# Attention heads of a graph layer: exponentials copied by DMA into float32r tiles and transposed from there, ScalarE's order changed

## The chip, the cores and the metric

The kernel runs on one core of one Trainium2 chip. The metric is the device time of one execution in microseconds, the median of several runs. A core has TensorE (PE, matmuls and transposes; its weight loads are shown apart as PEld), VectorE (DVE), ScalarE (ACT), GpSimd (POOL) and SyncE (SP), which here only issues DMAs. SP's DMAs go through one queue over the core's 16 DMA engines.

## What is computed

A two-layer graph attention network over 1,250 nodes with 768 features, then a feed-forward block. All in float32. The stage that the change touches is the attention of the first layer, with 8 heads of 128 channels:

```
h = (layernorm(x) @ W1.T).reshape(n, 8, 128)
e = leaky_relu(a_src[src] + a_dst[dst], 0.2)        # per edge and head
ex = exp(e - segment_max(e, dst)[dst])
alpha = ex / (segment_sum(ex, dst)[dst] + 1e-16)
h1 = relu(segment_sum(alpha[:, :, None] * h[src], dst) + b1)
```

The second layer does the same with one head of 768 channels on `h1 @ W2.T`; the block behind it is a normalisation and two matmuls with a GELU, and for six rows a routed variant.

## The kernel before, in words

The edges are first counted into a dense 1,250 x 1,250 matrix of log counts, `LC`. A head is then dense work on 10 row tiles of 125 destination nodes by 1,250 source nodes: the segment sum is a matmul of the features with the transposed matrix of exponentials.

The head stage walks over 40 pairs of row tiles (8 heads of 5 pairs; `NG` is 5, `n` counts pairs through all heads, `hh` counts head pairs). What is done for one pair k is spread over the steps of four engines:

- DVE, `logits` (L1824, L1832): for each of the two tiles, source logit plus destination logit with the leaky ReLU into `L[r]`, then adding `LC` with the row maximum; L1836 makes the negated maxima. Four tiles `L` serve two pairs. Then `reciprocals` of pair k-1 and `multiply` (L1860) of pair k-3.
- ACT: `evac` of pair k-1 (L828, five copies of 500 columns from PSUM into `PT`), then `exp` of pair k (L815, in place in `L[r]`, with row sums), `rdb_copy` of pair k-2 (L845), `relu` of pair k-4 into `hT` (L856).
- PE: `turn_bank` of pair k-1 (L1219: 20 transposes of 125 x 125, each a weight load of a block of `L` and a pass of the identity, into five PSUM banks), `spread` of pair k-2 (L1256, two transposes), `aggregate` of pair k-2 (L1240: 10 float32 matmuls, which the profile shows as 20, features `h1s` against `PT`).
- SP: a load of the next head's source logits (`load_logits`, L442, into `asb`, 1,250 KB) and of its features (`load_features`, L437, into `h1s`, 560 and 65 KB).

All order is written out by hand; engines meet only at semaphores: `exp_done` (exponentials of a pair), `tb_full` (a bank turned), `tb_evac`, `agg_done`, `mul_done`. An `L` tile is free for the pair after next when its pair is turned:

```
                    if not (first and k < 2):
                        dve.wait_ge(tb_full, NG * n + -NG)
```

Around the stage, SP's list holds six loads of `w2n_sb` (L409, 512 KB each) just before the head loop, and the load of `w2_sb` (L479, 3,072 KB), the second layer's weights, just behind it. In the stage's sixth step (the seventh pair's logits) PE multiplies `w2n_sb` (L1275). After pair 39 ACT splits `w2_sb` into a high part (L881, 8 casts), then does the last `rdb_copy` and `relu` and makes the first tiles `h1Tt_hi` (L885); PE starts the second layer on them (L1311).

## Time and profile before

| | us |
|---|---|
| median of 3 runs | 733.01 (731.76 to 735.08) |
| profiled execution, span | 730.7 |
| PE busy in the span | 718.9 |
| DVE busy | 518.6 |
| ACT busy | 390.7 |

The profile is one execution; its span runs from the first to the last instruction, and nothing else of its own time is recorded. Busy times of the page are shares of the whole span. Three views are used below: windows (busy time of each engine in a stretch), the timeline (instructions in order of time, like neighbours merged), and one line's or all lines' instructions with their lengths. In timeline rows the first number is the start, the second the length of the merged stretch; "x20" is the count. Times are microseconds from the span's start, mean lengths nanoseconds.

### The profile page before, as it was taken

What the parts mean: (1) busy time and instruction counts of PE and PEld (TensorE: products, weight loads), DVE (VectorE), ACT (ScalarE), POOL (GpSimd) and SP (SyncE); (2) the same over time, 40 slices, a digit from 0 to 9 for tenths busy, and PEclk for the clock granted to TensorE, in tenths of its full rate; (3) what the DMA queues carried; (4) which work ended last, traced back from release to release, by engine and by line L of the source; (5) the groups of instructions that cost most, each with busy time, mean ns of one, the idle gap of its engine ahead of it and who ended that gap; (6) DMA issues with size and microseconds to landing.
All of it is one profiled execution on the core that took longest, in us unless ns stands there. A gap on an engine that the chain in (4) does not pass through costs nothing.

```text
span 730.7 us, 13048 instructions
## 1 busy us (share of the span) xinstructions
PE 718.9 (98%) x4607; PEld 655.4 (90%) x4607; DVE 518.6 (71%) x940; ACT 390.7 (53%) x749; POOL 112.2 (15%) x95
## 2 busy tenths in 40 slices
PE   8899999999999999999999999999999999999998
PEld 6699999789899999999999999999999898978965
DVE  5899888699999999999999452336567543717141
ACT  4665574388698889888888931122231413322100
POOL 2569330000000000000000000000233330222211
PEclk9999999999999999999999999999999999999999
DMA  8627655759121221302230020001873544215011
GB/s 284 206 81 213 190 165 153 191 164 333 37 71 36 71 61 45 105 21 85 76 132 0 0 57 1 1 0 36 259 255 90 174 136 156 92 61 175 22 37 49
DMA packets 39665, 78.92 MB, mean 108 GB/s; under 512 B 4074, under 2 KB 25392, under 8 KB 38721
## 3 DMA queue, kind: packets, MB, share of 16 engines
q1 hardware_dynamic: 33932, 60.53, 27.2%
q10 hardware_dynamic: 4500, 13.82, 5.8%
q0 software_dynamic: 1184, 3.92, 1.8%
q8 instruction: 30, 0.49, 0.3%
q14 instruction: 19, 0.15, 0.1%
HBM read 62.97 MB, written 15.29 MB: 107 GB/s over the span
## 4 chain that ended last, share of the span: by engine, by line
PE 94%; DMA 3%; ACT 1%; DVE 1%; issue 0%; ACTq 0%; SPq 0%; POOL 0%; POOLq 0%; DVEq 0%
PE bank L1240 23%; PE bank L1382 15%; PE bank L1219 12%; PE bank L1311 12%; PE bank L1117 11%; PE bank L1458 5%; PE bank L1478 5%; DMA w1n_sb<-in_W 3%; PE bank L1034 3%; PE bank L1363 1%; PE bank L1256 1%; PE bank L1036 1%; PE bank L1430 1%; PE bank L1446 1%; PE bank L1049 1%; PE bank L1493 1%
## 5 line engine op out<-in xcount | busy, mean ns | idle before, releaser
L1240 PE MATMUL bank<-PT,h1s 125*128 125x250 f32 x800 | 175.8, 374 | 0.0
L1240 PEld LDWEIGHTS bank<-PT,h1s 125*128 125x128 f32 x800 | 148.5, 190 | 15.7
L1824 DVE SCALAR_TENSOR_TENSOR L<-asb,nadh 125x1250 f32<-125x1250 f32 x80 | 118.0, 1517 | 3.1 <-PE bank L1219 1.3
L828 ACT COPY PT<-bank 125x500 f32<-125x500 f32 x200 | 99.8, 596 | 37.8 <-PE bank L1219 37.8
L1832 DVE CUSTOM_DVE_ANT_0 L<-L,LC 125x1250 f32<-125x1250 f32 x80 | 113.4, 1455 | 0.0
L815 ACT ACTIVATE L<-L,nm 125x1250 f32<-125x1250 f32 x80 | 107.8, 1371 | 0.0
L1219 PEld LDWEIGHTS bank<-ident,L 125*125 125x125 f32 x800 | 93.3, 189 | 3.9 <-ACT L L815 1.5
L1219 PE MATMUL bank<-ident,L 125*125 125x125 f32 x800 | 94.6, 273 | 0.7 <-ACT L L815 0.7
L2005 DVE TENSOR_TENSOR x2f<-bank,x2f 125x384 f32<-125x384 f32 x20 | 10.3, 552 | 63.4 <-PE bank L1478 63.4
L1641 DVE TENSOR_TENSOR hotr<-iota,r 125x1500 f16<-125x1500 f16 x50 | 46.5, 931 | 8.0 <-PE bank L1036 4.4
L646 POOL MEMSET pick<- 128x90 f32 x1 | 0.2, 168 | 277.8 <-ACT hT L856 277.8
L1382 PE MATMUL bank<-h_hi,PT_hi 125*125 125x384 f32 x200 | 42.1, 352 | 0.0
L890 ACT CAST h_hi<-bank 125x384 f32 (+1 forms) x20 | 8.6, 483 | 59.6 <-PE bank L1311 59.6
L1382 PE MATMUL bank<-h_lo,PT_hi 125*125 125x384 f32 x200 | 40.4, 341 | 0.0
L916 ACT ACTIVATE L<-L,nm 125x1250 f32<-125x1250 f32 x10 | 13.4, 1339 | 50.3 <-DVE nm L1969 50.2
L1900 DVE COPY as2c<-bank 125x1 f32<-125x1 f32 x10 | 1.6, 158 | 54.4 <-ACT h_hi L890 54.4
L1478 PE MATMUL bank<-fc_sb,gT 128*125 128x384 f32 x120 | 40.2, 486 | 0.0
L1458 PE MATMUL bank<-yT,fc_sb 128*128 128x250 f32 x180 | 39.2, 375 | 0.7 <-ACT yT L930 0.7
L1382 PE MATMUL bank<-h_hi,PT_lo 125*125 125x384 f32 x200 | 38.3, 337 | 0.0
L1458 PEld LDWEIGHTS bank<-yT,fc_sb 128*128 128x128 f32 x180 | 33.8, 189 | 5.1 <-ACT yT L930 0.9
L1382 PEld LDWEIGHTS bank<-h_hi,PT_hi 125*125 125x125 f32 x200 | 34.0, 186 | 3.4 <-issue 0.8
L621 POOL TENSOR_TENSOR x<-x,b_sb 125x768 f32<-125x768 f32 x10 | 19.4, 1941 | 104.0 <-DMA fc2b_sb<-in_fc2b 94.4
(247 smaller groups left out, 1238.9 us busy)
## 6 DMA issues: line engine op xcount, KB each, us to landing
asb<-src_logit_rows SPq DMA_DIRECT2D x7, 1250.0 KB, 5.9
atom_w<-in_atom_inT SPq DMA_DIRECT2D x5, 1152.0 KB, 11.3
atom_w<-in_atom_outT SPq DMA_DIRECT2D x5, 1152.0 KB, 9.6
log_count_scratch<-LCw SPq DMA_DIRECT2D x10, 546.9 KB
LC<-log_count_scratch SPq DMA_DIRECT2D x10, 546.9 KB
LCt<-log_count_scratch SPq DMA_DIRECT2D x10, 546.9 KB
h_scratch<-h1st ACTq DMA_DIRECT2D x10, 448.0 KB
h1s<-h_scratch SPq DMA_DIRECT2D x7, 560.0 KB
```

The lines of the kernel that those rows point to most:

```text
L815: e = act.activation(L[r][:, :], L[r][:, :], ACT.Exp, bias=nm[q][:, t:t + 1], scale=1.0, accum_out=den[q][:, t:t + 1])
L828: act.copy(PT[(k - lag) % 2][:, 2 * b:2 * b + 2, :], bank[turned_bank(first, k - lag, b)][0:NP, 0:2 * GW].rearrange("p (s n) -> p s n", s= ...
L1117: mm = pe.matmul(bank[b][0:NP, 0:c1 - c0], rows[t % 2][:, k, :], weights[:, k, c0:c1], start=(part == 0 and k == 0), stop=(part == 2 and k ...
L1219: mm = pe.transpose(bank[turned_bank(first, k - lag, b)][0:NP, (2 * s + j) * NP:(2 * s + j + 1) * NP], L[(2 * (k - lag) + j) % 4][:, (2 * ...
L1240: mm = pe.matmul(bank[2 + (k - lag) % 2][:, 0:GW], h1s[q][:, s, :], PT[(k - lag) % 2][:, s, :], start=(s == 0), stop=(s == NT - 1))
L1311: mm = pe.matmul(bank[2 * p + b][0:NP, 0:w], rows[p][:, k, :], weights[:, k, c0:c0 + w], start=(part == 0 and k == 0), stop=(part == 2 and ...
L1382: mm = pe.matmul(bank[2 + 2 * j + b][0:NP, 0:HALF], rows[:, s, j * NP:(j + 1) * NP], features[:, s, b * HALF:(b + 1) * HALF], start=(term ...
L1458: mm = pe.matmul(bank[6 + m // 2][:, (m % 2) * GW:(m % 2 + 1) * GW], fc1_sb[:, k, m * 128:(m + 1) * 128], yT[:, k, :, :].rearrange("p j n ...
L1478: mm = pe.matmul(bank[down_bank(i, j) + b][0:NP, 0:HALF], gT[:, m, j * NP:(j + 1) * NP], fc2_sb[:, m, b * HALF:(b + 1) * HALF], start=(m = ...
L1641: dve.tensor_tensor(hotr[w][:, :, :, :], iota2[:, 0:GW, :].unsqueeze(1).to_broadcast([CE, TRIP, GW, 2]), r16[:, ds(2 * pair, 2 * TRIP)].re ...
L1824: dve.scalar_tensor_tensor(L[r][:, :], asb[q][0:NP, 1, :], nadh[q][:, t:t + 1], asb[q][0:NP, 0, :], ALU.add, ALU.max).then_inc(stt_done, 1)
L1832: dve.tensor_tensor_reduce(out=L[r][:, :], in0=L[r][:, :], in1=LC[:, t, :], scale=1.0, scalar=-3e38, op0=ALU.add, op1=ALU.max, accum_out=m ...
```

## The change

From pair 2 on, SP copies each tile of exponentials, bits unchanged, into one of four new tiles `Lr` of type float32r, with two DMAs for a tile (rows 0 to 111 and 112 to 124). PE turns the blocks from there, with a float32r identity and 126 columns, since `Lr` has a 126th row, which POOL sets to zero once. The first two pairs are turned as before. PE and DVE wait for the copy (`copied`) where they waited for the exponentials and for the turn. `exp_done` is counted per tile. ACT does `exp` of pair k ahead of `evac` of pair k-1 (not in the first three steps). The loads of logits and features are issued by SP between copies. Some tiles move in memory to make room.

```diff
+EVEN = NP + 1
...
+PAIR = 2 * TWO
+PLAIN = 2
...
+        ident_r = sb("ident_r", [128, 128], F32R)
...
-        wrow2 = sb("wrow2", [2, HC], F32, p3)
-        pad3 = sb("pad3", [128, 4064], F32, p3)
+        Lr = [sb(f"Lr{r}", [EVEN, N], F32R, p3) for r in range(4)]
+        pad3 = sb("pad3", [128, 80], F32, p3)
...
+        once = ExitStack()
+        sb("pad_hT", [C, (H - 1) * N], F32, once)
+        wrow2 = sb("wrow2", [2, HC], F32, once)
+        once.close()
...
-            with sp.Fori(0, H // 2 - 1) as hh:
-                for q in range(2):
-                    sp.wait_ge(stt_done, NT * (2 * hh + q) + NT)
-                    load_logits(q, 2 * hh + q + 2)
-                    sp.wait_ge(agg_done, NG * (2 * hh + q) + NG)
-                    load_features(q, 2 * hh + q + 2)
+            def copy_pair(hh, k):
+
+                n = 2 * NG * hh + k
+                for j in range(2):
+                    r = (2 * k + j) % 4
+                    sp.wait_ge(exp_done, 2 * n + (j + 1))
+                    if j == 0:
+                        sp.wait_ge(tb_full, NG * n + -NG)
+                    for a, b in ROWS:
+                        sp.dma_start(Lr[r][a:b, :].bitcast(F32), L[r][a:b, :]).then_inc(copied[k % 2], 16)
+
+            def copy_heads(hh, first=False, last=False):
+                for k in range(PLAIN if first else 0, 2 * NG):
+                    copy_pair(hh, k)
+                    if k == 1 and not first:
+                        sp.wait_ge(agg_done, 2 * NG * hh)
+                        load_features(1, 2 * hh + 1)
+                    if k == NG - 1 and not last:
+                        load_logits(0, 2 * hh + 2)
+                    if k == NG + 1 and not last:
+                        sp.wait_ge(agg_done, 2 * NG * hh + NG)
+                        load_features(0, 2 * hh + 2)
+                    if k == 2 * NG - 1 and not last:
+                        load_logits(1, 2 * hh + 3)
+
+            sp.wait_ge(spare_row, len(Lr))
+            copy_heads(0, first=True)
+            with sp.Fori(1, H // 2 - 1) as hh:
+                copy_heads(hh)
+            copy_heads(H // 2 - 1, last=True)
             sp.wait_ge(wattp, 3)
             sp.dma_start(w2_sb[:, :, 0:D], W2T.rearrange("(k p) n -> p k n", p=128)).then_inc(w2_in, 16)
@@ -611,6 +647,10 @@
...
+            pool.wait_ge(h1_full, NT)
+            for r in range(4):
+                pool.memset(Lr[r][96:EVEN, :].bitcast(F32), 0.0).then_inc(spare_row, 1)
...
@@ -812,9 +852,8 @@
                 act.wait_ge(nm_ready, n + 1)
                 for j in range(2):
                     r, t = (2 * k + j) % 4, 2 * g + j
-                    e = act.activation(L[r][:, :], L[r][:, :], ACT.Exp, bias=nm[q][:, t:t + 1], scale=1.0,
-                                       accum_out=den[q][:, t:t + 1])
-                e.then_inc(exp_done, 1)
+                    act.activation(L[r][:, :], L[r][:, :], ACT.Exp, bias=nm[q][:, t:t + 1], scale=1.0,
...
-                    act.copy(PT[(k - lag) % 2][:, 2 * b:2 * b + 2, :],
-                             bank[turned_bank(first, k - lag, b)][0:NP, 0:2 * GW].rearrange("p (s n) -> p s n", s=2)
-                             ).then_inc(tb_evac, 1)
+                    act.copy(PT[(k - lag) % 2][:, 2 * b:2 * b + 2, :].rearrange("p s (j n) -> p (s j) n", j=2),
+                             bank[turned_bank(first, k - lag, b)][0:NP, 0:4 * EVEN]
+                             .rearrange("p (q n) -> p q n", q=4)[:, :, 0:NP]).then_inc(tb_evac, 1)
...
             def step(hh, k, **at_end):
-                evac(hh, k, **at_end)
+                early = at_end.get("first") and k <= PLAIN
+                if early:
+                    evac(hh, k, **at_end)
                 exp(hh, k, **at_end)
+                if not early:
+                    evac(hh, k, **at_end)
                 rdb_copy(hh, k, **at_end)
                 relu(hh, k, **at_end)
 
 
             for k in range(2 * NG):
                 step(0, k, first=True)
+                if k == 0:
+                    act.wait_ge(wattp, 1)
+                    act.copy(ident_r[:, :], ident[:, :]).then_inc(ident_done, 1)
...
-                if b == 0:
-                    pe.wait_ge(exp_done, n + 1)
+                plain = first and k - lag < PLAIN
+                if b == 0 and plain:
+                    pe.wait_ge(exp_done, 2 * n + 2)
+                elif b == 0:
+                    pe.wait_ge(copied[(k - lag) % 2], PAIR * NG * hh + PAIR * ((k - lag) // 2))
+                if first and k == lag + PLAIN and b == 0:
+                    pe.wait_ge(ident_done, 1)
...
                 for s in range(2):
                     for j in range(2):
-                        mm = pe.transpose(bank[turned_bank(first, k - lag, b)][0:NP, (2 * s + j) * NP:(2 * s + j + 1) * NP],
-                                          L[(2 * (k - lag) + j) % 4][:, (2 * b + s) * NP:(2 * b + s + 1) * NP],
-                                          ident[0:NP, 0:NP])
+                        r, at0, width = (2 * (k - lag) + j) % 4, (2 * s + j) * EVEN, NP if plain else EVEN
+                        block = slice((2 * b + s) * NP, (2 * b + s + 1) * NP)
+                        turned = bank[turned_bank(first, k - lag, b)][0:NP, at0:at0 + width]
+                        if plain:
+                            mm = pe.transpose(turned, L[r][:, block], ident[0:NP, 0:NP])
+                        else:
+                            mm = pe.transpose(turned.bitcast(F32R), Lr[r][:, block], ident_r[0:EVEN, 0:EVEN])
                 mm.then_inc(tb_full, 1)
...
                 for j in range(2):
                     r, t = (2 * k + j) % 4, 2 * g + j
-                    if not (first and k < 2):
+                    if first and 2 <= k < 2 + PLAIN:
                         dve.wait_ge(tb_full, NG * n + -NG)
+                    elif not first or k >= 2:
+                        dve.wait_ge(copied[k % 2], PAIR * NG * hh + PAIR * (k // 2 - 1))
                     elif k == 1:
                         dve.wait_ge(lc_stored[0], TWO * NG)
...
-                dve.wait_ge(exp_done, n + 1)
+                dve.wait_ge(exp_done, 2 * n + 2)
```

The order on SP at the head stage's start, before (the rows are DMAs in order of issue, tile written, tile read and shape; ISA rows compute wait values):

```order
L442 DMA asb<-src_logit_rows 128x2500
L437 DMA h1s<-h_scratch 112x10x128
L437 DMA h1s<-h_scratch 13x10x128
L409 DMA w2n_sb<-in_W 128x1024 x6
L472 UNCONDITIONAL_BRANCH
L472 ISA
L442 ISA
L442 DMA asb<-src_logit_rows 128x2500
```

and now:

```order
L454 DMA asb<-src_logit_rows 128x2500
L449 DMA h1s<-h_scratch 112x10x128
L449 DMA h1s<-h_scratch 13x10x128
L421 DMA w2n_sb<-in_W 128x1024 x6
L493 DMA Lr<-L 112x1250
L493 DMA Lr<-L 13x1250
L493 DMA Lr<-L 112x1250
L493 DMA Lr<-L 13x1250
```

The copies of pair 2 follow the six loads of `w2n_sb`; the next load of `asb` comes after the copies of pairs 2, 3 and 4.

At the stage's end, SP before:

```order
L437 DMA h1s<-h_scratch 13x10x128
L472 REGISTER_ALU
L472 COMPARE_AND_BRANCH
L479 DMA w_sb<-in_W2T 128x8x768 [waits wattp]
L492 DMA LCt<-log_count_scratch 112x1250 [waits lc_stored0,relu_done,lc_stored1,mul_done,agg_done]
```

and now:

```order
L493 DMA Lr<-L 112x1250 [waits tb_full,exp_done]
L493 DMA Lr<-L 13x1250
L493 DMA Lr<-L 112x1250 [waits exp_done]
L493 DMA Lr<-L 13x1250
L515 DMA w_sb<-in_W2T 128x8x768 [waits wattp]
```

The load of `w2_sb` stood behind the last load of features; it stands behind the copies of all pairs up to the last.

## Rows read from the trace of the kernel before

**Rows 1.** Page, part 1: busy time, share of the span, instructions.

```profile
PE 718.9 (98%) x4607; PEld 655.4 (90%) x4607; DVE 518.6 (71%) x940; ACT 390.7 (53%) x749; POOL 112.2 (15%) x95
```

**Rows 2.** Windows; columns: busy of each engine, granted clock, DMA share, GB/s.

```profile
380.00:400.00 20.00, 20.00 (x129) 18.68 (x129) 19.68 (x34) 17.47 (x35) 0.00 (x0) 1.00 0.00 0
```

**Rows 3.** Timeline, one pair of the head stage, all engines.

```profile
398.41 2.34 PE L1219 MATMUL bank<-ident,L 125*125 125x125 f32 x20
399.91 0.17 DVE L1836 TENSOR_SCALAR nm<-mx 125x2 f32<-125x2 f32 x1
400.79 2.95 DVE L1824 SCALAR_TENSOR_TENSOR L<-asb,nadh 125x1250 f32<-125x1250 f32 x2
400.80 4.39 PE L1240 MATMUL bank<-PT,h1s 125*128 125x250 f32 x20
401.38 1.38 ACT L815 ACTIVATE L<-L,nm 125x1250 f32<-125x1250 f32 x1
405.03 2.34 PE L1219 MATMUL bank<-ident,L 125*125 125x125 f32 x20
```

**Rows 4.** Timeline, DVE: three multiplies in a row.

```profile
301.23 0.42 DVE L1860 TENSOR_TENSOR tmp<-bank,rdb 128x250 f32<-128x250 f32 x1
307.68 0.42 DVE L1860 TENSOR_TENSOR tmp<-bank,rdb 128x250 f32<-128x250 f32 x1
314.45 0.42 DVE L1860 TENSOR_TENSOR tmp<-bank,rdb 128x250 f32<-128x250 f32 x1
```

**Rows 5.** Weight loads: timeline of L1151, line L1281, groups L1382 and L1219.

```profile
35.23 1.44 PEld L1151 LDWEIGHTS bank<-watt,xT_first 128*125 128x125 f32 x12
L1281 PEld LDWEIGHTS bank<-ident,wrow x8: 136/137/139, 199.0 to 199.4; 2*128 2x128 f32 x8
L1382 PEld LDWEIGHTS bank<-h_hi,PT_hi 125*125 125x125 f32 x200 | 34.0, 186 | 3.4 <-issue 0.8 <-ACT PT_hi L924 0.7
L1219 PEld LDWEIGHTS bank<-ident,L 125*125 125x125 f32 x800 | 93.3, 189 | 3.9 <-ACT L L815 1.5 <-issue 0.4 <-ACT h1st L717 0.2
```

**Rows 6.** Timeline of SP for one tile and one logit load; windows of three loads.

```profile
589.72 0.76 SPq L492 DMA_DIRECT2D LCt<-log_count_scratch  x2
304.69 0.35 SPq L442 DMA_DIRECT2D asb<-src_logit_rows  x1
306.00:310.00 4.00, 4.00 (x31) 3.80 (x30) 3.78 (x9) 3.71 (x8) 0.00 (x0) 1.00 0.83 320
327.00:330.00 3.00, 3.00 (x20) 2.80 (x20) 2.85 (x6) 3.00 (x7) 0.00 (x0) 1.00 0.85 212
590.50:593.50 3.00, 3.00 (x19) 3.00 (x18) 0.00 (x0) 0.62 (x1) 0.00 (x0) 1.00 0.75 208
```

**Rows 7.** Start of the stage: SP's timeline, landing of asb loads, PE's third turn.

```profile
165.27 3.67 SPq L409 DMA_DIRECT2D w2n_sb<-in_W  x6
169.33 0.35 SPq L442 DMA_DIRECT2D asb<-src_logit_rows  x1
DMA to landing us min/median/max: 5.7/5.9/14.9
162.59 2.45 PE L1219 MATMUL bank<-ident,L 125*125 125x125 f32 x20
```

**Rows 8.** End of the stage: w2_sb load and its landing, ACT's split, PE's second layer.

```profile
360.15 0.40 SPq L479 DMA_DIRECT2D w_sb<-in_W2T  x1
DMA to landing us min/median/max: 12.0/12.0/12.0
415.29 6.00 ACT L881 CAST w_hi<-w_sb 128x770 fp32r<-128x770 f32 x8
423.53 3.08 PE L1311 MATMUL bank<-w_hi,h1Tt_hi 128*125 128x384 f32 x16 [0.65 <-DVE tmp L1860]
```

**Rows 9.** Timeline of PE, start of the kernel.

```profile
1.54 5.25 PE L996 MATMUL bank<-ident 128*128 128x128 f32 x26 [1.54 <-POOL ident L571]
8.42 1.48 PE L996 MATMUL bank<-ident 128*128 128x128 f32 x12
```

More of the change, by code:

```diff
@@ L135, in gnn_ffn_kernel @@
         att2 = sb("att2", [128, 2, KD])
-        attz = sb("attz", [C, H, 2 * H])
+        once = ExitStack()
+        attz = sb("attz", [C, H, 2 * H], F32, once)
+        once.close()
+        ident_r = sb("ident_r", [128, 128], F32R)
         watt1 = sb("watt1", [128, KD, 2 * H])
@@ L267, in gnn_ffn_kernel @@
         rdb = [sb(f"rdb{i}", [C, GW], F32, p3) for i in range(2)]
-        wrow2 = sb("wrow2", [2, HC], F32, p3)
-        pad3 = sb("pad3", [128, 4064], F32, p3)
+        Lr = [sb(f"Lr{r}", [EVEN, N], F32R, p3) for r in range(4)]
+        pad3 = sb("pad3", [128, 80], F32, p3)
         PT = [sb(f"PT{s}", [NP, NT, GW], F32, p3) for s in range(2)]
+        once = ExitStack()
+        sb("pad_hT", [C, (H - 1) * N], F32, once)
+        wrow2 = sb("wrow2", [2, HC], F32, once)
+        once.close()
         hT = sb("hT", [C, H, N], F32, p3)
@@ L349, in gnn_ffn_kernel @@
         cnt_full, ln_done, lc_done = (sem(n) for n in ("cnt_full", "ln_done", "lc_done"))
-        lc_in = [sem(f"lc_in{t}") for t in range(NT)]
+        lc_in = [sem(f"lc_in{g}") for g in range(NG)]
         lc_stored = [sem(f"lc_stored{p}") for p in range(2)]
@@ L358, in gnn_ffn_kernel @@
         exp_done, tb_full, tb_evac, agg_done = (sem(n) for n in ("exp_done", "tb_full", "tb_evac", "agg_done"))
+        ident_done, spare_row = sem("ident_done"), sem("spare_row")
+        copied = [sem(f"copied{p}") for p in range(2)]
         dn_done, rden_ready, rdb_full, rdb_ready = (sem(n) for n in ("dn_done", "rden_ready", "rdb_full", "rdb_ready"))
@@ L405, in load_lc @@
                 for a, b in ROWS:
-                    sp.dma_start(LC[a:b, t, :], lc_d[t * NP + a:t * NP + b, :]).then_inc(lc_in[t], 16)
+                    sp.dma_start(LC[a:b, t, :], lc_d[t * NP + a:t * NP + b, :]).then_inc(lc_in[t // 2], 16)
             def load_w2n(k):
@@ L814, in exp @@
                     r, t = (2 * k + j) % 4, 2 * g + j
-                    e = act.activation(L[r][:, :], L[r][:, :], ACT.Exp, bias=nm[q][:, t:t + 1], scale=1.0,
-                                       accum_out=den[q][:, t:t + 1])
-                e.then_inc(exp_done, 1)
+                    act.activation(L[r][:, :], L[r][:, :], ACT.Exp, bias=nm[q][:, t:t + 1], scale=1.0,
+                                   accum_out=den[q][:, t:t + 1]).then_inc(exp_done, 1)
             def evac(hh, k, first=False, last=False):
@@ L1828, in logits @@
                     dve.wait_ge(stt_done, 2 * n + (j + 1))
-                    if first and k < NG:
-                        dve.wait_ge(lc_in[t], TWO)
+                    if first and k < NG and j == 0:
+                        dve.wait_ge(lc_in[g], PAIR)
                     alone(dve)
```

## The prediction, made before the change was run

> **What bounds the kernel now.** I read the page first: PE is busy 98% of the 730.7 us span [rows 1]. That is an average over stages, so I then cut the head stage (about 149 to 423 us, 40 pairs of row tiles) into windows: PE is busy 20.00 us of 20, DVE 19.7, ACT 17.5 [rows 2]. Two engines stand at the limit, and a faster PE is worth only what the second one allows.
>
> One pair in order of time [rows 3]: PE turns pair k-1 (20 transposes, start 398.41), spreads, aggregates pair k-2 (4.39 us), and turns the next at 405.03. The period is 6.62 us and PE has no gap: 20 transposes and 2 spreads make 2.4 (398.41 to 400.80), the 20 matmuls 4.23 (to 405.03). DVE's first logit of the pair starts 0.04 us after a turn ends (398.41 + 2.34 = 400.75, then 400.79), so in this stretch DVE is released by PE. What DVE would need alone is seen where it isn't [rows 4]: from 301.23 to 307.68 is 6.45 us. Once per five pairs a small copy lifts that to 6.77 (307.68 to 314.45) [rows 4], mean 6.51. **The head stage can gain at most 0.12 us a pair while DVE's work stays as it is**: 36 pairs, 4.3 us, plus 0.9 us in the last turn.
>
> **Do the transposes get faster?** A transpose is a weight load (the 125 columns of a block) and a moving pass (the identity). The change halves at most the moving pass. Twelve matmuls with 125-column weights and only 16 moving columns still take (1.44 - 0.19)/11 = 0.114 us each [rows 5]: the load of 125 columns alone paces them. Today's 20 transposes and 2 spreads go at 0.109 (398.41 to 400.80) [rows 3], and a load of 125 float32r columns is as long as one of float32, 0.186 against 0.189 us [rows 5]. So both passes of today's transpose cost 0.11 us, and shortening one leaves the other: I take no gain on PE. The other bound is about 0.06 us each, eight starts from 199.0 to 199.4, from loads of 128 columns in float32 transposes, each 0.137 long [rows 5]; 125 columns remain 125 in the change, so the 125-column rows are the nearer. The Trainium skill (TensorE: Matmul & The Clock Gate, "LDWEIGHTS (loading the stationary operand)") makes the load cost its columns over 1.2, here 104 ns, whatever the type. By that rule the turns stay as they are. The trace agrees at 125 float32 columns, and disagrees at 128 columns in a transpose.
>
> **Copy and its deadline.** Before, the turn needs only the exponentials; now it needs a landed copy. Let N be the time at which a pair's maxima are ready. With ACT taking exponentials first they end at N+1.35 and N+2.65 (1.38 us for one [rows 3]; today they start at 401.38 for N = 399.91 + 0.17, 1.3 us later, since ACT was copying; that gain is part of the deadline below). If DVE runs ahead as far as it can, it waits to multiply the aggregate of pair k-3; the chain pair's copy, turn (6.63 us PE step), multiply, two logit passes (6.5 us) spans three periods. So with a copy landing at N+L, 3P = L + 13.13, and P stays 6.63 for L up to 6.76; the other chain, copy to reuse of L, is 2P = L + 6.2. Price of L: one tile of this shape (112 and 13 rows of 5,000 bytes) is loaded from DRAM with issue at 589.72 and its last data at about 593.5, 3.8 us [rows 6]. The signal follows the last data by about 0.6 us (the 1,250 KB load: data to 310.0, landing 304.69 + 5.9 = 310.6) [rows 6, 7]. Second tile: 2.65 + 3.8 + 0.6 = 7.05. Lateness of 0.3 us over three periods is 0.1 a pair, 3.6 us in all; at 400 instead of 320 GB/s it is nothing.
>
> **Copies share SP's queue with the loads.** Six loads of the source logits (4.0 us of data at 320 GB/s) and six of the features (3.0 us at 212 GB/s) [rows 6] now stand between copies. A pair's two tiles are 1.28 MB, 4.0 us of data at 320 GB/s and 3.2 at 400. Behind a logit load a pair ends 1.4 us late (slow) or 0.1 (fast), behind a feature load 2.0 or 1.25. PE has no gap to absorb it: 12 events make 20 or 8 us. With the line above: 8 to 24 us; I take 14. The Trainium skill (DMA: Bandwidth & Descriptors, "Anatomy of one DMA") gives 2.0 us plus bytes over 436e3 per DMA, 4.9 us for 1.28 MB. The trace has 5.9 for that size from DRAM; by the page the low end, 8 us, would hold, 774 us in total.
>
> **The first copy.** SP issues the six w2n loads (3 MB) from 165.27 to 168.9, and the copy of pair 2 comes behind them (the order of SP above) [rows 7]. Today the 1,250 KB load of asb stands at exactly that place: issued at 169.33, it lands 14.9 us later, at 184.2 [rows 7]. The copies of pair 2 are also 1,250 KB. Today pair 2 is turned at 162.59, with no gap before it [rows 7]. PE would wait until 184.2: **+21.6 us**. Nothing after it makes this up: DVE has logits of pairs 2 and 3 done by then and no free L for pair 4.
>
> **The weights of the second layer.** SP issues w2_sb (3 MB, 12.0 us to landing) at 360.15, 55 us before ACT splits it (415.29, 6.00 us) [rows 8]. In the change it stands behind the copy of the last pair. The last pair's turn starts at 405.03 + 6.62 = 411.65 today [rows 3], so N = 411.65 - 6.75 = 404.9 (shifted as all before it); exponentials end at +2.65, SP's issues add 0.85: 408.4. Landing: 12.0, plus 1.7 behind the copies: 422.1. Splitting ends at 428.1, then two ACT steps and the first tile of hT as today (421.3 to 423.5, 2.2 us): PE starts the second layer at 430.3 instead of 423.53 [rows 8]: **+6.8 us**.
>
> **Restarts of a cold PE.** PE idles some 21 us and some 7 us. At the kernel's start 26 transposes take 5.25 us, 0.202 each, and 12 later ones 1.48, 0.123 each [rows 9]. In the head stage the granted clock reads 1.00 (2.4 GHz) [rows 2] and a transpose takes 0.109, so the first 26 ran at about half of that. I take 26 x 0.079 = 2.1 us per restart, 4.2 in all. (Bounds: 0 and 8.)
>
> Small: the ident_r copy and POOL's four memsets lie before the first float32r turn, at engines that wait (no price if done by 184); one more issue of SP costs 0.35 us, inside the 0.85. PSUM copies by ACT keep their 500 columns.
>
> **Sum.** 730.7 + 21.6 + 6.8 + 4.2 + 14 = 777.3 against the span. The median of the runs is 2.3 us above the span (733.01): **780 us**.
>
> **Rivals.**
> - B: transposes at 0.06 us. The PE step is 5.7 us, DVE is the bound with 6.51. The first stall stays; from there DVE's chain counts: last N at 406.7 + 19.5 (its own delay) - 4.2 - 1.0 (waits on PE near 187 and 202 us gone) = 421.0, second layer 25.4 later, at 446.4 instead of 423.5: +22.9. With 2.1 for one cold start and some 9 of queueing, 765 + 2.3: 767 us. For it: 128-column loads. Against it: every 125-column float32 and float32r load.
> - C: copies are slower than DRAM loads and land at N+9. Then 2P = 15.2, P = 7.6: 36 x 0.97 = 35 us in place of the 14: 801 us. For it: nothing measured, SBUF to SBUF isn't in this trace. Against: 320 GB/s and more in all large loads.
> - D: the rings don't hold the copy of pair 2 behind the w2n loads but serve both in turns: it lands some 8 us after its exponentials, near 170, and 15 us are saved: 765 us. Against: the asb load in that place waited.
> - E, the other side: the period follows PE at 5.7 us, 38 x 0.93 = 35 us less, without the queueing 14: 730.7 + 21.6 + 6.8 + 4.2 - 35 = 728.3 in the span, 731 in the runs: not slower. It decides when DVE's work per pair falls below 5.7 us; it takes 6.45 where nothing holds it [rows 4], and the change takes nothing off it.
> - The change doesn't do what it says (types alone, no speed): that is my forecast for the transposes, not for the copies.
>
> **How the numbers follow.** Forecast 0.50, B 0.25, C 0.12, D 0.10, E 0.03. Range 758 to 798: the low end takes in B and D with the fast copies, the high end most of C and the slow queueing (790). A measurement of this kernel tells about 0.5% (3.7 us) from no change: faster than that 0.03, within it 0.03, slower 0.94.
>
> **What would show it.** Transposes per turn still about 2.3 us (B: 1.4). PE idle of some 20 us before the third turn, ended by DMA Lr<-L, the last w2n load landing just before. SP's w2_sb issue some 3.5 us after the last maxima and ACT's split waiting for it. A period of 6.6 to 6.8 us in quiet pairs, longer where a load of asb or h1s lies ahead of a copy. Wrong if the third turn comes before 175 us, if quiet pairs take over 7.2 us, or if the second layer isn't held by w2_sb.

## The result, and the profile after

| | before | after |
|---|---|---|
| median | 732.39 us (731.76 to 735.08, 4 runs) | 835.24 us (833.62 to 836.91, 4 runs) |
| profiled span | 730.7 | 835.1 |
| mean granted clock in the span | 0.999 | 0.943 |

The ratio is 1.140, 95% interval 1.137 to 1.143: 14% slower. The forecast was 780 us, 758 to 798: the sign was right, but it had 48 us of a loss of 103.

The page of the changed kernel, against [rows 1] and the group of L1219 in [rows 5]:

```profile
PE 755.8 (91%) x4607; PEld 683.1 (82%) x4607; DVE 520.2 (62%) x940; ACT 396.2 (47%) x750; POOL 115.7 (14%) x99
...
PEclk9999999967979797979898999999999999999999
...
L1276 PE MATMUL bank<-ident_r,Lr 126*125 126x126 f32 x760 | 108.0, 304 | 61.5 <-DMA Lr<-L 61.5
L1276 PEld LDWEIGHTS bank<-ident_r,Lr 126*125 126x125 f32 x760 | 102.3, 216 | 69.1 <-issue 39.1
L1881 DVE SCALAR_TENSOR_TENSOR L<-asb,nadh 125x1250 f32<-125x1250 f32 x80 | 117.9, 1516 | 49.5 <-DMA Lr<-L 48.7
```

TensorE has the same 4,607 instructions, but is busy 36.9 us longer, and idle (span less busy) 67.5 us longer: that is the whole 104.4 us. Its wait has a name, the copy. The row of the clock (40 slices of the span) says why it is also busier: the clock falls again and again all through the head stage, to a mean of 0.89 from 190 to 510 us.

TensorE's waits of over 1 us from 20 to 560 us (engine, line, what it waited for: us in total, times, longest):

```profile
PE bank L1276 <- DMA Lr<-L: 61.5, 14, 24.1
PE bank L1366 <- ACT h1Tt_hi L931: 5.1, 1, 5.1
PE bank L1214 <- DMA w1n_sb<-in_W: 2.6, 1, 2.6
```

The start of the head stage, timeline, against [rows 7]; then the end, against [rows 8]:

```profile
168.90 4.09 SPq L421 DMA_DIRECT2D w2n_sb<-in_W  x6
173.11 27.09 SPq L493 DMA_DIRECT2D Lr<-L  x11
190.34 4.46 PE L1276 MATMUL bank<-ident_r,Lr 126*125 126x126 f32 x20 [24.15 <-DMA Lr<-L]
...
509.91 2.40 PE L1276 MATMUL bank<-ident_r,Lr 126*125 126x126 f32 x20
...
518.12 5.98 ACT L927 CAST w_hi<-w_sb 128x770 fp32r<-128x770 f32 x8 [4.37 <-DMA w_sb<-in_W2T]
526.34 3.87 PE L1366 MATMUL bank<-w_hi,h1Tt_hi 128*125 128x384 f32 x12 [5.12 <-ACT h1Tt_hi L931]
```

The third turn starts at 190.34 instead of 162.59: 24.15 us of wait, and 3.6 us that this execution had already lost before (2.0 of it in L1214's wait for w1n_sb, 2.6 us here, 0.6 in the kernel before, 0.5 to 2.7 in the other runs). From the third turn to the last it is 319.57 us instead of 249.06. With the 2.77 us for w2n_sb taken off, 37 periods make **8.56 us a pair** instead of 6.66. From the last turn to the second layer it is 16.43 us instead of 11.88. The 70.5 us between the third turn and the last are the largest part of the loss: TensorE waits 37.4 of them, before thirteen turns, and is busy 33.2 longer (windows: 282.2 us of 319.57, before 249.06 of 249.06).

One wait in the middle, timeline (the row at 354.82 ends the maxima of the pair whose copy is awaited; a load of `h1s` is issued just ahead of that copy):

```profile
354.82 0.17 DVE L1893 TENSOR_SCALAR nm<-mx 125x2 f32<-125x2 f32 x1
...
356.24 0.94 SPq L449 DMA_DIRECT2D h1s<-h_scratch  x2
...
357.40 19.17 SPq L493 DMA_DIRECT2D Lr<-L  x11
...
366.58 2.95 DVE L1881 SCALAR_TENSOR_TENSOR L<-asb,nadh 125x1250 f32<-125x1250 f32 x2 [3.42 <-DMA Lr<-L]
366.68 4.45 PE L1276 MATMUL bank<-ident_r,Lr 126*125 126x126 f32 x20 [3.98 <-DMA Lr<-L]
...
377.75 2.48 PE L1276 MATMUL bank<-ident_r,Lr 126*125 126x126 f32 x20
```

The windows of that stretch (busy of each engine, granted clock, DMA share, GB/s):

```profile
362.00:366.00 4.00, 0.70 (x4) 0.29 (x2) 0.93 (x6) 2.75 (x4) 0.00 (x0) 0.98 0.99 256
366.00:372.00 6.00, 5.32 (x24) 5.25 (x25) 5.42 (x5) 3.14 (x7) 0.00 (x0) 0.50 0.61 167
```

The copy lands 11.6 us after its maxima (366.58 - 354.99), TensorE waits 3.98 us, and then turns in 4.45 us what takes 2.4 to 2.5 otherwise: the clock reads 0.50, 1.2 GHz, and the next turn comes 11.1 us later instead of 6.6. Such a wait is paid twice.

That holds for seven of the fourteen waits for a copy: 24.15, 3.75, 4.70, 3.64, 3.98, 4.25 and 3.61 us. After each of them the next turn comes 9.5 to 11.1 us later, together 26.6 us over seven periods of 6.6. The other seven waits are 1.50 to 2.30 us long, and only two of them (2.19 and 1.77 us) cost clock, 1.6 us each. The last short waits, timeline (`...` stands for other instructions):

```profile
479.79 2.52 PE L1276 MATMUL bank<-ident_r,Lr 126*125 126x126 f32 x20 [1.77 <-DMA Lr<-L]
...
487.96 2.48 PE L1276 MATMUL bank<-ident_r,Lr 126*125 126x126 f32 x20
...
494.56 2.48 PE L1276 MATMUL bank<-ident_r,Lr 126*125 126x126 f32 x20
...
503.01 2.39 PE L1276 MATMUL bank<-ident_r,Lr 126*125 126x126 f32 x20 [1.50 <-DMA Lr<-L]
```

The places are regular too. The six waits of 3.6 to 4.7 us stand before the turns of pairs 7, 12, 17, 22, 27 and 32, whose copies SP issues right behind a load of `h1s`. Five of 1.8 to 2.3 us stand before pairs 10, 15, 20, 25 and 30, whose copies follow a load of `asb`. Only two, the 1.77 and 1.50 us above (pairs 35 and 38), have no load ahead of them. From pair 34 to 39 SP issues no load of `asb` or `h1s`, and the pairs take 7.8 us each ((509.91 - 471.08)/5; 7.45 without the one stretch of slow clock), against 8.7 us in the 32 pairs before (w2n_sb taken off).

### The profile page after: what moved, and what is told of

The parts are those of the page before. It is cut to its first block, busy times and chain, and to the rows that moved or that the text cites. A ratio compares the mean times of both kernels' runs of the same rounds, so it can differ in the third digit from the quotient of the medians.

```text
span 835.1 us, 13227 instructions
## 1 busy us (share of the span) xinstructions
PE 755.8 (91%) x4607; PEld 683.1 (82%) x4607; DVE 520.2 (62%) x940; ACT 396.2 (47%) x750; POOL 115.7 (14%) x99
## 4 chain that ended last, share of the span: by engine, by line
PE 74%; DMA 15%; SPq 5%; issue 2%; ACT 2%; DVE 1%; ACTq 0%; POOL 0%; DVEq 0%; POOLq 0%
PE bank L1437 13%; PE bank L1295 13%; PE bank L1366 10%; DMA Lr<-L 10%; PE bank L1276 10%; PE bank L1163 9%; PE bank L1513 5%; PE bank L1533 4%; SPq L493 4%; DMA w1n_sb<-in_W 3%; PE bank L1080 2%; DMA w_sb<-in_W2T 1%; PE bank L1418 1%; PE bank L1311 1%; PE bank L1082 1%
## 5 line engine op out<-in xcount | busy, mean ns | idle before, releaser
L1295 PE MATMUL bank<-PT,h1s 125*128 125x250 f32 x800 | 189.5, 394 | 0.0
L1295 PEld LDWEIGHTS bank<-PT,h1s 125*128 125x128 f32 x800 | 159.6, 204 | 19.3
L1276 PE MATMUL bank<-ident_r,Lr 126*125 126x126 f32 x760 | 108.0, 304 | 61.5 <-DMA Lr<-L 61.5
L1276 PEld LDWEIGHTS bank<-ident_r,Lr 126*125 126x125 f32 x760 | 102.3, 216 | 69.1 <-issue 39.1
L867 ACT COPY PT<-bank 125x500 f32<-125x500 f32 x200 | 101.9, 585 | 68.5 <-PE bank L1276 66.8
L1917 DVE TENSOR_TENSOR tmp<-bank,rdb 128x250 f32<-128x250 f32 x40 | 16.8, 419 | 56.5 <-PE bank L1295 53.3
L962 ACT ACTIVATE L<-L,nm 125x1250 f32<-125x1250 f32 x10 | 13.4, 1339 | 50.6 <-DVE nm L2026 50.5
```

Source lines behind the costliest of these rows:

```text
L867: act.copy(PT[(k - lag) % 2][:, 2 * b:2 * b + 2, :].rearrange("p s (j n) -> p (s j) n", j=2), bank[turned_bank(first, k - lag, b)][0:NP, 0 ...
L1276: mm = pe.transpose(turned.bitcast(F32R), Lr[r][:, block], ident_r[0:EVEN, 0:EVEN])
L1295: mm = pe.matmul(bank[2 + (k - lag) % 2][:, 0:GW], h1s[q][:, s, :], PT[(k - lag) % 2][:, s, :], start=(s == 0), stop=(s == NT - 1))
```

## The experiments

Times are medians; the kernel before gave 731.3 to 732.0 us beside them.

### ScalarE's order alone, in the kernel before

```diff
-                evac(hh, k, **at_end)
+                early = at_end.get("first") and k <= 2
+                if early:
+                    evac(hh, k, **at_end)
                 exp(hh, k, **at_end)
+                if not early:
+                    evac(hh, k, **at_end)
```

> The kernel before with one part of the change alone: ScalarE takes the exponentials of a pair ahead of its copies of the pair before (not in the first three steps). My theory (the loss is all in the copies): within 3 us of the kernel before, 730 to 736 us; PE stays busy 98% of the span. Rival 1, the order alone costs: the copies out of PSUM come 2.7 us later in each step, TensorE waits for a bank or for PT, and each of 40 pairs gets up to 0.5 us longer: 740 to 750 us. Rival 2, it gains: exponentials 1.3 us earlier let VectorE's 6.51 us set the period, 4 us less: 728 to 730 us.

739.01 us, ratio 1.011 (1.008 to 1.014): 7 us of loss, outside of my theory's 730 to 736 and 1 us short of rival 1's range. The mechanism is rival 1's. The timeline shows a loop over two pairs:

```profile
398.87 0.17 DVE L1840 TENSOR_SCALAR nm<-mx 125x2 f32<-125x2 f32 x1
...
401.73 2.46 ACT L828 COPY PT<-bank 125x500 f32<-125x500 f32 x5
...
404.24 2.26 PEld L1223 LDWEIGHTS bank<-ident,L 125*125 125x125 f32 x20 [0.27 <-ACT PT L828]
404.24 2.45 PE L1223 MATMUL bank<-ident,L 125*125 125x125 f32 x20
...
406.72 2.95 DVE L1828 SCALAR_TENSOR_TENSOR L<-asb,nadh 125x1250 f32<-125x1250 f32 x2 [0.22 <-PE bank L1223]
...
411.07 1.06 PEld L1223 LDWEIGHTS bank<-ident,L 125*125 125x125 f32 x9 [0.33 <-ACT PT L828]
```

Maxima, two exponentials, five copies out of PSUM, turn, logits and the next maxima (they end at 412.64) take 13.6 us for two pairs, 6.8 a pair (404.24 to 411.07 is 6.83): the turn now waits for copies that stand behind the exponentials.

### The order undone, in the changed kernel

The same two lines turned back. What was open by then is told in the expectation.

> The changed kernel with ScalarE's order as before: the copies out of PSUM first, then the exponentials, in every step. The prediction booked the new order as 1.3 us of gain on the copy's way; alone it cost 7 us in the kernel before. If the landing after the maxima decides (the chain maxima, exponentials, copy, turn, multiply, logits), the copy starts up to 2.5 us later where ScalarE has copies to do, and the mean period grows by a third to a half of that: 840 to 865 us. If the DMA engines' time for 1.22 MB a pair is the bound, and not the chain, an earlier or later start changes little: 830 to 840 us.

**993.18 us**: neither range. In this order the exponentials of pair k stand behind copies that wait for the turn of pair k-1, which waits for its DMA. The loop of exponentials, DMA, turn and PSUM copies closes in one pair instead of two: 13.4 us from one turn (406.63) to the next (420.07). So the order costs 7 us where nothing needs it, and without it the DMA could not be hidden at all. It also gives the cleanest landing, since no load is near (timeline, then windows of 1 us):

```profile
411.55 1.34 ACT L855 ACTIVATE L<-L,nm 125x1250 f32<-125x1250 f32 x1
...
412.88 1.33 ACT L855 ACTIVATE L<-L,nm 125x1250 f32<-125x1250 f32 x1
413.10 3.34 SPq L493 DMA_DIRECT2D Lr<-L  x4
...
419.97 1.52 DVE L1877 SCALAR_TENSOR_TENSOR L<-asb,nadh 125x1250 f32<-125x1250 f32 x1 [2.64 <-DMA Lr<-L]
```

```profile
414.00:415.00 1.00, 1.00 (x7) 0.89 (x6) 0.33 (x2) 0.95 (x4) 0.00 (x0) 1.00 0.78 230
415.00:416.00 1.00, 1.00 (x7) 0.89 (x6) 0.00 (x0) 0.00 (x0) 0.00 (x0) 1.00 0.92 295
416.00:417.00 1.00, 0.78 (x4) 0.37 (x2) 0.09 (x1) 0.00 (x0) 0.00 (x0) 1.00 0.91 290
417.00:418.00 1.00, 0.00 (x0) 0.00 (x0) 0.33 (x1) 0.00 (x0) 0.00 (x0) 1.00 0.97 300
418.00:419.00 1.00, 0.00 (x0) 0.00 (x0) 0.00 (x0) 0.00 (x0) 0.00 (x0) 1.00 0.52 130
```

From the first exponential to the landing it is 8.4 us, so L, the time from a pair's maxima to its landed copy, is 8.5 where 7.05 was forecast; pair 38 of the changed kernel, with no load near, has the same (maxima at 494.59, turn at 503.01). The rate of 290 to 300 GB/s was near the 320 that I took. From the second exponential's end (414.21) to the release it is 5.76 us instead of 3.8 + 0.6. The trace divides it: SP begins the second tile's DMAs 0.43 us late (414.64), since it is still at the first tile's, and is done with them at 416.44. All but some 5 KB have moved by 419.0 and those by 419.4 (13 GB/s for 0.4 us), so the second tile takes 4.4 to 4.8 us from its first issue to its last data instead of 3.8. The release follows 0.6 to 1.0 us behind, about as forecast.

### The copies as traffic only

TensorE and VectorE don't wait for them; `LC` is the source, since it is not overwritten.

```diff
-                plain = first and k - lag < PLAIN
+                plain = True
...
-                        sp.dma_start(Lr[r][a:b, :].bitcast(F32), L[r][a:b, :])
+                        sp.dma_start(Lr[r][a:b, :].bitcast(F32), LC[a:b, 2 * (k % NG) + j, :])
```

> The copies as mere traffic: the same four DMAs a pair into the same float32r tiles, but read from LC, and neither TensorE nor VectorE waits for them; all transposes read L in float32 as before. SP paces them by the exponentials and by the landing of the pair two before. The loads keep the order of the changed kernel. The output is the reference's, since the copied tiles are not read. My theory (the loss is the wait for the copy, not what the traffic does to the engines): TensorE keeps 6.6 us a pair and a granted clock of 1.00, nothing waits before the third turn; only w2_sb is late as in the changed kernel, 5 to 7 us: 737 to 742 us. Rival 1, traffic in SBUF slows VectorE, ScalarE or TensorE: DVE's logit pass of 2 x 1,250 columns grows from 2.95 us and the period passes 7 us: 750 us or more. Rival 2, the loads of asb and h1s come late behind the copies and hold DVE and PE at each head: 745 to 760 us, with waits for asb or h1s in front of every fifth pair.

751.15 us, above my 737 to 742. But the period is 6.77 to 6.83 us, that of ScalarE's order alone (739 us), and a logit pass of two tiles still takes 2.95 us: traffic slows no engine, and nothing waits for `asb` or `h1s`, so the mechanisms of rivals 1 and 2 fall although rival 1's "750 us or more" came. Between the spans (750.1 and 737.1 us) lie 9.1 us of wait for w2_sb ahead of the second layer, 2.6 of slow clock behind it, and 1.2 of wait for w2n_sb.

> The copies as mere traffic, once more, but read from the log counts in DRAM instead of from the same numbers in LC in SBUF: the same bytes, rows and issues into the same tiles. With the source in SBUF the 16 DMA engines moved 240 to 250 GB/s at a busy share of 1.00 all through the head stage (751 us). If a source in SBUF is what makes the copies slower than the 320 GB/s of the loads from DRAM on which the forecast rested, the same bytes now take a share of 0.75 to 0.85, the load of w2_sb comes sooner, and the time falls to 740 to 746 us. If the rate hangs on the row length or on the destination alone, the share stays at 1.00 and the time at 751 us.

747.71 us (one execution), neither number. One line of SP and one window of each, source in SBUF, then in DRAM:

```profile
L494 SPq DMA_DIRECT2D Lr<-LC x152: 529/797/1827, 169.5 to 418.1; - x152
...
250.00:300.00 50.00, 49.75 (x312) 44.85 (x311) 47.48 (x76) 42.32 (x80) 0.00 (x0) 1.00 0.98 251
```

```profile
L494 SPq DMA_DIRECT2D Lr<-log_count_scratch x152: 303/390/677, 167.2 to 415.2; - x152
...
250.00:300.00 50.00, 49.74 (x306) 44.74 (x305) 47.79 (x74) 42.54 (x82) 0.00 (x0) 1.00 1.01 253
```

The rate doesn't hang on the source. The issue does: 0.80 us at the median from SBUF, 0.39 from DRAM. And at this demand, 1.25 MB of copies and 0.38 MB of loads a pair in 6.8 us, the 16 engines have hardly a gap.

### Fewer bytes, fewer issues

```diff
-                        sp.dma_start(Lr[r][a:b, :].bitcast(F32), L[r][a:b, :])
+                        sp.dma_start(Lr[r][a:b, 0:N // 2].bitcast(F32), L[r][a:b, 0:N // 2])
```

> The changed kernel with half of each copy left out: only the first 625 of 1,250 columns of each tile are copied (the rest of Lr stays zero, so the attention of the first layer is computed from half of its sources). The number of DMAs and their rows stay, the bytes halve. Theory 1, the copies' bytes set the landing (the ring moves some 245 to 250 GB/s, 5 us for a pair): the landing comes 2.5 us sooner, quiet pairs fall to the 6.8 us of the kernel with ScalarE's order alone, TensorE seldom waits for Lr and keeps its clock; with the stalls at the start (some 20 us) and at w2_sb (8 us) left: 765 to 775 us. Theory 2, SP's issue of four DMAs a pair sets it (0.79 us each at the median, 3.2 us a pair): the time stays over 815 us. If an issue takes longer only because the ring is full, the median issue falls below 0.6 us here.

775.05 us, with half of each tile left out: the bytes, as theory 1 has it, with a period of 7.03 us ((447.00 - 184.18 - 2.77)/37) and a clock of 0.98 in the stage. The start and the second layer keep their waits (22.1 and 5.2 us). An issue still takes 0.71 us at the median, so it isn't long only because the engines are behind.

> The changed kernel with one DMA for a tile in place of two: rows 0 to 111 are copied, rows 112 to 124 are not (those 13 rows of each tile stay zero, which is left out of the first layer's sums). Half the issues, 10% fewer bytes. By the bytes (theory 1) the landing comes 0.5 us sooner, 0.17 to 0.25 us a pair over 37 pairs, 6 to 9 us, and some slow clock: 820 to 828 us. By the issues (theory 2) two issues of 0.79 us less put the landing 1.6 us sooner: 25 us and the slow clock of the waits that go, 790 to 805 us.

811.99 us, with 13 rows of each tile left out, period 7.98: a larger gain than a tenth of the bytes was to give (820 to 828), a smaller one than theory 2 wanted (790 to 805). I read it as issues and bytes both on the copy's way; the run changes both at once.

```profile
L493 SPq DMA_DIRECT2D Lr<-L x76: 511/512/1104, 169.7 to 479.5; - x76
```

Then the same number of issues with all 125 rows in one DMA (`for a, b in ((0, NP),)`), in the changed kernel and in the one with four mends (below):

> The changed kernel with each tile copied by one DMA of all 125 rows instead of two of 112 and 13 rows: the same bytes and output, half the issues. In a quiet pair of the last runs the landing came 5.8 us after the second exponential's end, where the forecast had 4.4; two issues of 0.79 us stood in it, where the forecast had 0.38 each as for a source in DRAM. Theory, issue time is on the copy's way: the landing comes 0.8 to 1.6 us sooner, the two-pair loop (2P = L + 6.2) gives back 0.4 to 0.8 us a pair and some slow clock: 800 to 820 us. Rival, 125 rows spread unevenly over 16 engines (eight rows on some instead of seven, or fewer engines): the data takes longer and the time stays at 830 us or grows.

> The kernel with the four mends (811.5 us), and one DMA of 125 rows for each tile. If issue time is on the way of each copy: 0.4 to 0.8 us a pair of 36, 15 to 29 us, and the slow clock of the waits that go: 775 to 795 us. If 125 rows spread badly: 811 us or more.

**974.18 and 920.09 us**: the rival, in a size that I hadn't thought of. Copies run one behind the other without a gap, at a third of the engines:

```profile
410.00:412.00 2.00, 2.00 (x6) 1.67 (x5) 0.00 (x0) 2.00 (x3) 0.00 (x0) 0.50 0.31 128
...
420.00:422.00 2.00, 2.00 (x11) 1.80 (x10) 1.97 (x6) 0.03 (x1) 0.00 (x0) 1.00 0.32 130
```

A share of 0.31 is 5 of 16. The Trainium skill (DMA: Bandwidth & Descriptors, "Why a DMA increments its semaphore by 16 and not by 1") has a DMA use the largest number up to 16 that divides its rows: 5 for 125, 16 for 112. By that rule, the trace agrees. So this pair of runs says nothing on the price of an issue, which stays without a number of its own.

### The loads and the start

w2n_sb loaded in the count stage, w2_sb in eight pieces behind the copies of the last two heads:

> The changed kernel with the two big loads out of the copies' way: the six w2n_sb loads are issued in the count stage, before the last two tiles of LC are stored, and w2_sb is loaded in eight pieces of 384 KB, one behind the copies of each of the first eight pairs of the last two heads. My theory (each stall has its own place and goes when its load goes): the 24 us wait before the third turn falls to under 4 us, the slow clock behind it (4.46 + 6.16 us instead of 2.34 + 4.39, 3.9 us) goes too, TensorE's 5.1 us wait before the second layer and its 1.5 us of slow clock go: 835 - 22 - 4 - 6.5 = 803 us, with a mean period of the pairs still at 8.5 us. Rival 1, the pieces of w2_sb delay eight copies by 1.3 us each (384 KB at 300 GB/s) and the earlier w2n loads delay the tiles of LC: some 10 us back, 813 us. Rival 2, the third turn waits for something else (POOL's zeroing, the identity, the copies' own 8 us): the wait stays over 10 us, 820 us or more.

818.91 us, with rival 2's wait. The second layer waits 0.63 us again, but the third turn still waits 15.8 us:

```profile
165.72 22.90 SPq L494 DMA_DIRECT2D Lr<-L  x12
177.93 4.46 PE L1279 MATMUL bank<-ident_r,Lr 126*125 126x126 f32 x20 [15.79 <-DMA Lr<-L]
```

Pair 2's exponentials end at 161.95, but SP stands in the stores and loads of LC and in asb and h1s until 165.72. From there the copy takes 12.2 us to land, with the DMA engines at a share of 1.03 to 1.10 (165 to 175 us). The w2n loads were only 8.4 of the 24.15 us.

> The kernel with the two big loads moved (818.9 us), and the first four pairs turned from L in float32 instead of the first two, so that the first copy is that of pair 4. There the third turn still waits 15.8 us for a copy that SP issues at 165.7 us, behind stores and loads of LC, asb and h1s, and that lands at 177.9 us, and then runs at the slow clock (4.46 and 5.46 us instead of 2.5 and 4.4). Theory: what is left of the stall at the start is this queue; by pair 4 it has drained, and the wait is the copy's own lateness of one pair, 1 to 3 us: 818.9 - 13.5 - 3 = 802 us. Rival: the wait moves to pair 4 whole: 815 us or more.

812.55 us. The first wait falls to 5.1 us, but the period of the other 35 pairs is 8.8 us instead of 8.6; between theory and rival.

> The changed kernel with the six loads of asb and six of h1s inside the head stage issued from ScalarE's queue instead of SP's, at about the same steps (the loads of features one step later). Only copies stand in SP's queue between pairs 2 and 39. Theory 1, the loads cost by standing in front of the copies in one queue: copies no longer end late behind them, the waits of 3 to 5 us behind them go and with them the slow clock; 12 events of 4 us and more: 790 to 805 us. Theory 2, the 16 DMA engines are shared by both queues, and a copy that runs beside 1.25 MB of loads ends as late as one behind it: 825 to 840 us.

833.89 us, period 8.56 again: theory 2. The loads don't cost by their place in SP's list; what is left is the time of the DMA engines that they take. No run takes them away.

### All mends together

> All four mends of the copies together: w2n_sb and w2_sb loaded elsewhere, copies from pair 4 on, blocks of 126 columns, loads of asb and h1s from ScalarE's queue. By the chain of prediction (a copy that lands at N + L sets 3P = L + 13.1, less 0.5 for the shorter turn; 2P = L + 6.2) and a quiet landing of 7.5 to 8.4 us, the period is 6.8 to 7.1 us, against 6.83 that ScalarE's order alone gives: 739 + 0 to 10 us: 739 to 750 us. Rival: the mean period stays over 7.5 us since the waits for copies are of their own kind and not behind loads: 765 us or more.

811.50 us, the rival: 8.7 us a pair. The chain that I had used gave 6.8 to 7.1. A pair of it, timeline:

```profile
200.95 0.17 DVE L1917 TENSOR_SCALAR nm<-mx 125x2 f32<-125x2 f32 x1
...
212.50 2.95 DVE L1905 SCALAR_TENSOR_TENSOR L<-asb,nadh 125x1250 f32<-125x1250 f32 x2 [4.13 <-DMA Lr<-L]
212.52 2.77 PE L1300 MATMUL bank<-ident_r,Lr 126*126 126x126 f32 x20 [5.55 <-DMA Lr<-L]
```

11.4 us from the maxima to the landing. ScalarE had issued the load of h1s at 201.57, and the next pair's first exponential was ready at 208.95, so its copy was on its way too: three transfers share the engines. With L = 8.5 undisturbed, 2P = L + 6.2 (P is the period of a pair) leaves no slack, 7.35 us against 6.83. My reading is that everything that shares then adds in full; the traces agree with it, no run isolates it.

### The price of waiting

In the changed kernel, ten transposes of the identity ahead of each wait:

> The changed kernel, with ten more transposes of the identity (125 x 125, 0.109 us each, 1.1 us a pair) ahead of each wait of TensorE for a copy; what they write is overwritten by the turn. A test of the price of the slow clock: in the changed kernel the same instructions keep TensorE busy 755.8 us instead of 718.9, of which the turns of 2.48 us explain 5. Theory A, waiting costs twice, since the clock falls to its lower level behind each wait of some 4 us: the filled waits are shorter, some stay under the point where the clock falls, and the added 41 us are more than half given back: 825 to 845 us with a mean clock over 0.96 (0.943 in the changed kernel). Theory B, the slow clock follows from something else (the load of the chip, the DMA traffic): the clock stays at 0.94 and the time goes up by the part of the 41 us that doesn't fall into waits, to 850 us or more.

831.81 us: 41 us of work added, 3 us less time. Theory A.

```profile
PE 778.3 (94%) x4987; PEld 711.7 (86%) x4987; DVE 519.9 (63%) x940; ACT 396.4 (48%) x750; POOL 111.8 (13%) x99
...
PE bank L1279 <- DMA Lr<-L: 35.4, 8, 25.5
```

Without the first wait (25.5) there are 10 us in seven waits, where the changed kernel has 37 in thirteen, and the mean clock is 0.963 instead of 0.943.

### 126 columns, and no copies

```diff
+                            block = slice(block.start, block.stop + 1)
```

> The changed kernel with one size changed: the block that is loaded as weights has 126 columns instead of 125 (the tiles Lr are 1,252 wide), the moving side stays 126. My theory for the transposes (the load of the weights paces them, at about one column in 1.2 GHz whatever the type): a turn stays at 2.4 us, the load at about 189 ns, the time at 835 us within 5. Rival 1, the odd column count was what kept the load slow, as the eight loads of 128 columns of the kernel before (137 ns, a pitch of 0.06 us) hint: the turn falls to 1.3 us, the load to about 140 ns, and since the copy's chain is shorter by 1.1 us in three periods, the time falls by 0.35 us x 37 pairs = 13 us, and some slow clock less: 815 to 825 us.

823.34 us, rival 1. Loads and one turn:

```profile
L1280 PEld LDWEIGHTS bank<-ident_r,Lr x760: 136/141/183, 185.3 to 497.1; 126*126 126x126 f32 x190
...
495.54 1.88 PE L1280 MATMUL bank<-ident_r,Lr 126*126 126x126 f32 x20 [0.55 <-DMA Lr<-L]
```

One more column takes the load from 189 to 141 ns and the turn from 2.39 to 1.88 us behind a short wait, from 2.48 to 1.99 elsewhere. The Trainium skill (TensorE: Matmul & The Clock Gate, "LDWEIGHTS (loading the stationary operand)") has the load grow with its columns, 105 against 104 ns; the trace has it fall, and decides.

Then the float32r tiles without any copy. ScalarE, which writes the exponentials anyway, writes them there:

```diff
-                    act.activation(L[r][:, :], L[r][:, :], ACT.Exp, ...
+                    act.activation(Lr[r][0:NP, :], L[r][:, :], ACT.Exp, ...
...
-                        dve.wait_ge(copied[k % 2], PAIR * NG * hh + PAIR * (k // 2 - 1))
+                        dve.wait_ge(exp_done, 2 * n + -2)
```

> The changed kernel without any copy: ScalarE writes the exponentials from L straight into the float32r tile Lr (for pairs 2 to 39), with the transposes of 125 x 126 as in the change; SP's loads are where they stand in the kernel before, VectorE may refill L as soon as the exponentials are read. My theory (all of the loss is the copies and their queue, plus 7 us from ScalarE's order, which falls here because L comes free before the turn): the head stage runs at TensorE's own 6.7 us a pair (a turn of 2.48 us against 2.34), 733 to 738 us. Rival 1: the order of ScalarE costs here as alone (6.83 us a pair): 739 to 742 us. Rival 2: VectorE runs ahead freely and TensorE, not being its releaser, still takes 6.6: 730 to 733 us.

731.86 us, ratio 0.9996 (0.9979 to 1.0012), rival 2: VectorE refills L as soon as ScalarE has read it, so the loop of the first experiment is gone too.

> As the kernel with exponentials written straight into float32r tiles, with blocks of 126 columns as weights (tiles 1,252 wide), whose turn took 1.9 us where it was tried with the copies, in place of 2.48. TensorE then needs 6.1 us a pair and VectorE 6.51 us, the period follows VectorE: 0.11 us a pair below the kernel before, 38 x 0.11 = 4 us, and 0.5 us in the last turn: 727 to 730 us, faster than both kernels. Rival 1: the small gaps before TensorE's turns cost clock: 735 us or more. Rival 2: ScalarE's order makes the loop maxima, exponentials, copies, turn the longest one, 2.6 + 2.5 + 1.9 and the rest hidden: 732 to 738 us.

**729.44 us, ratio 0.997 (0.995 to 0.998)**, the best version: 2.2 us under the kernel before. The group of the turns:

```profile
L1260 PE MATMUL bank<-ident_r,Lr 126*126 126x126 f32 x760 | 71.8, 250 | 8.2 <-ACT PT L850 5.5 <-ACT Lr L838 0.4 <-DVE wrow L1758 0.4
```

TensorE is busy 706.8 us, 12 less than before, but the span is only 3.5 us shorter (727.2 against 730.7): the turns now come mostly every 6.45 us, about once per five pairs 6.8, which is VectorE's pace as [rows 4] had it.

## Why the forecast was wrong, step by step

- **Transposes keep their pace: right.** 2.34 became 2.39 to 2.48 us. The reason given, that 125 columns of weights pace them, is right as far as it goes; that 126 are faster wasn't seen, though the 128-column rows in [rows 5] pointed there (rival B's row).
- **The first copy, +21.6: 24.15 measured**, the right place and size. The asb load in the same place [rows 7] carried the whole queue in its 14.9 us; the w2n loads, which the prediction named, were only a third of it.
- **w2_sb, +6.8: 6.0 measured**, 4.5 of wait (5.12 less the 0.65 of before) and 1.5 of slow clock.
- **Restarts, 4.2 for two: this step failed, in price and in count.** TensorE is busy 36.9 us longer with the same instructions. The longer turns don't make it: with the same transposes and no copies (ScalarE writing the float32r tiles itself, 731.86 us) TensorE is busy 717.8 us, against 718.9 before. It is the slow clock. One restart costs 3.8 us (the first: turn 4.46 for 2.48, aggregate 6.16 for 4.39), not 2.1. And there are seven behind waits for copies, two short ones of 1.6 us and the 1.5 us at the second layer, 31 us in all. The forecast had only its two large waits in mind.
- **Copy and its deadline, 14 us: the main failure.** The thirteen waits behind the third turn are 37.4 us. L = 7.05 was too short: it is 8.5 undisturbed and 11.6 behind a load of `h1s` (the wait at 366.68). The sum had SP free to issue the second tile as soon as its exponentials were done, and 3.8 us from there to its last data. By the formula of the prediction, 2P = L + 6.2, 8.5 alone gives 0.7 us a pair, 27 us; rival C was this mechanism, with 9 for L and 35 us, at 0.12. Then the loads: priced as a lateness of 0.1 to 2 us at twelve places, 8 to 20 us, they lengthen a chain that is already the bound. The places were right. But the eleven waits there are 34 us, and behind six of them come 3.8 us of slow clock each.
- **The sum, measured:** 24.2 for the first wait, 37.4 for the thirteen others, 6.0 at the second layer, 29.7 of slow clock between the third turn and the last and 3.6 before the stage make 100.9 of the 104.4 us. How the 37.4 divide between the longer L and the shared engines, the runs don't tell exactly.
- **Two inputs were off without effect.** A pair's two tiles are 1.25 MB, not 1.28. And the formula of the Trainium skill (DMA: Bandwidth & Descriptors, "Anatomy of one DMA — SWDGE (gpsimd) path"), 2.0 us plus bytes over 436e3, is a fit for DMAs that GpSimd issues. SP issues the ones here, so the sum was right to go by the trace.
- **ScalarE's order, a gain of 1.3 us: wrong as priced.** Alone it costs 7 us, by a loop through the PSUM copies that I never drew; with the copies it is what keeps the kernel from 993 us.
- **Rival D fell** (190 us, not 170). **"Quiet pairs take over 7.2 us"** was named as a sign against the forecast. Between the waits single turns do follow each other in 6.5 to 6.9 us, as forecast, because the loss gathers in one pair of the chain. But the only pairs with no load near, the last five, take 7.8 us each, 7.45 without their slow clock, so the sign came.

## What to carry to other kernels

Before a transfer is put between two engines of a stage without slack, draw each closed loop through it, in-order queues included, and add up the loop: by the formula of the prediction, 1.5 us more latency became 0.7 us a pair. Count the waits of TensorE one by one: here each of 3.6 us or more cost another 3.8 us in the clock after it. And if an engine writes the data anyway, let it write the type that the next one wants: the copy was not needed.

## What the hardware showed that I had not expected

- A float32r block of 126 columns loads faster than one of 125 (141 against 189 ns). Why isn't settled; only these two widths were run in float32r, and in float32 a load of 128 columns takes 137 ns ahead of the transposes of [rows 5] but 189 ns in the aggregate (L1240 of the kernel before), so the width alone doesn't decide it.
- A DMA of 125 rows runs on a share of 0.31 of the engines at 128 to 130 GB/s; cut at row 112, the same bytes go at 290 to 300.
- SP spends 0.80 us at the median on an issue with its source in SBUF, 0.39 with it in DRAM. From SBUF it is 0.51 where only the 112-row copies are issued.
- An undisturbed copy of two tiles took 5.76 us from the second tile's last exponential to its release; the release came 0.6 to 1.0 us after the last data.
- Traffic at a DMA share of 0.98 to 1.02 for 230 us (170 to 400 us of the run with traffic only) changed neither the turn (2.45 us) nor the logit pass (2.95) nor the exponential (1.34) against the run with ScalarE's order alone.
- Of fourteen waits of TensorE for a copy, all seven of 3.6 us and more were followed by the 1.2 GHz level, and two of the seven of 2.3 us and less.
